# An opening with one array of scalars and single tiles, shifts on GpSimd, and the first w2 in quarters

## What is computed

```python
x = x + tanh(g_xattn[0]) * wkv(time_decay, time_first, k=layernorm(x), v=ctx_2048)
x = x + tanh(g_ffn[0])   * moe(layernorm(x), Wg, bg, W1, W2)

def wkv(...):                     # per batch and channel, over 256 positions
    aa, bb = decay * aa + exp(k) * v, decay * bb + exp(k)   # in a stable form
    y = (aa + exp(u + k) * v) / (bb + exp(u + k))           # with the sums before this position

def moe(x, Wg, bg, W1, W2):       # 2048 tokens, 4 experts, H = 2048
    logits = x @ Wg + bg          # the best two experts of each token, softmax over them
    for i in range(4):            # each expert takes the 512 tokens with the highest probability
        out[sel] += (gelu(x[sel] @ W1[i]) @ W2[i]) * p[sel]
```

## Time and profile before

| | us |
|---|---|
| median of 3 runs | 503.39 (503.37 to 503.77) |
| the profiled execution | 503.8 |
| its span, first to last instruction | 501.9 |
| TensorE busy | 419.5 |
| VectorE busy | 318.8 |
| ScalarE busy | 251.1 |
| GpSimd busy | 110.5 |

### The profile page before, as it was taken

The page is one execution under the profiler, slowest core; times in us unless marked ns, Lnnn a source line. Parts: engine busy times, 40 slices in busy tenths (PEclk is TensorE's granted clock), DMA queues, the critical chain, the costliest instruction groups (busy, mean ns, idle before and its releaser), DMA issues.

```text
span 501.9 us, 7234 instructions
## 1 busy us (share of the span) xinstructions
PE 419.5 (84%) x2012; PEld 200.3 (40%) x2012; DVE 318.8 (64%) x611; ACT 251.1 (50%) x374; POOL 110.5 (22%) x118
## 2 busy tenths in 40 slices
PE   0667877731168999999999999999999999999992
PEld 0433343310034444444444445444444444444440
DVE  4999999978747996173678419268833827771000
ACT  3736588970744445790444677154477615540000
POOL 1756636661030001311100221110031210001111
PEclk9997889985559999999999999999999999999998
DMA  7974012088530802918300471910075120000221
GB/s 225 347 308 179 17 42 86 31 304 292 210 85 0 335 0 82 359 9 288 100 0 1 164 275 21 355 21 0 1 255 184 21 27 16 0 0 1 35 29 21
DMA packets 24690, 59.30 MB, mean 118 GB/s; under 512 B 3040, under 2 KB 3040, under 8 KB 22624
## 3 DMA queue, kind: packets, MB, share of 16 engines
q1 hardware_dynamic: 19072, 50.68, 27.0%
q0 software_dynamic: 3584, 8.39, 8.4%
q10 hardware_dynamic: 2016, 0.02, 0.2%
HBM read 46.50 MB, written 12.58 MB: 118 GB/s over the span
## 4 chain that ended last, share of the span: by engine, by line
PE 70%; DVE 15%; ACT 6%; issue 3%; POOL 1%; DVEq 0%; ACTq 0%; POOLq 0%
PE ps L616 33%; PE ps L631 33%; DVE arena L990 5%; DVE arena L1009 2%; ACT arena L776 2%; PE ps L585 1%; DVE arena L1020 1%; DVE arena L1206 1%; ACT early L758 1%; PE ps L579 1%; DVE bn L967 1%; ACT rows L691 1%; ACT early L683 1%; DVE arena L1005 1%; ACT arena L707 1%
## 5 line engine op out<-in xcount | busy, mean ns | idle before, releaser
L616 PE MATMUL ps<-arena,early 128*128 128x512 f16 x768 | 166.4, 379 | 1.3 <-ACT arena L782 1.3
L631 PE MATMUL ps<-arena 128*128 128x512 f16 x768 | 167.4, 379 | 0.0
L616 PEld LDWEIGHTS ps<-arena,early 128*128 x768 | 75.0, 98 | 92.0 <-issue 2.1
L631 PEld LDWEIGHTS ps<-arena 128*128 128x128 f16 x768 | 74.9, 98 | 88.6
L797 ACT ACTIVATE arena<-ps,up 128x512 f32<-128x512 f32 x64 | 44.0, 687 | 84.0 <-PE ps L616 81.3
L1332 DVE TENSOR_SCALAR arena<-ps,yscale 128x512 f32<-128x512 f32 x16 | 12.0, 749 | 82.7 <-PE ps L631 61.3
L927 POOL DMA_INDIRECT result<-arena,idx x16 | 26.0, 1624 | 160.1 <-DVE arena L1332 158.5
L792 ACT ACTIVATE arena<-rows,down x64 | 45.6, 712 | 30.1 <-PE ps L631 30.1
L1317 DVE SCALAR_TENSOR_TENSOR arena<-arena,h_down 128x512 f32 x64 | 48.1, 751 | 9.7 <-DVE arena L1315 0.8
L1292 DVE SCALAR_TENSOR_TENSOR early<-w_raw,down,early 128x2048 f16<-128x2048 f32 x16 | 36.9, 2345 | 23.9 <-ACT early L758 22.3
L918 POOL DMA_INDIRECT arena<-xn_table,idx x16 | 17.1, 1069 | 158.5 <-DVE plist L1275 154.9
(11 more groups left out here) (160 smaller groups left out, 368.7 us busy)
## 6 DMA issues: line engine op xcount, KB each, us to landing
w_raw<-in_L_ffn_W SPq DMA_DIRECT2D x4, 4096.0 KB, 13.8
rows<-in_L_ffn_W SPq DMA_DIRECT2D x4, 4096.0 KB, 16.4
rows<-in_x SPq DMA_DIRECT2D x3, 1024.0 KB, 10.0
result<-rows SPq DMA_DIRECT2D x3, 1024.0 KB, 6.1
early<-in_ctx SPq DMA_DIRECT2D x4, 512.0 KB, 6.8
early<-in_ctx SPq DMA_DIRECT2D x2, 1024.0 KB, 6.6
xn_table<-arena SPq DMA_DIRECT2D x4, 512.0 KB, 3.5
xn_table<-arena SPq DMA_DIRECT2D x2, 1024.0 KB, 4.3
```

The lines of the kernel that those rows point to most:

```text
L616: last = nc.tensor.matmul(ps[:, PH[q], :], w[:, k, at], t[:, k, :], start=n == 0, stop=n == 3 * CT - 1)
L631: last = nc.tensor.matmul(ps[:, PY[s % 2], :], h[:, t, s * P:(s + 1) * P], w[:, t, :], start=t == 0 and n == 0, stop=t == HT - 1 and n == 2)
```

## The change

- **Opening.** All small inputs come in one array of 30 columns, laid out on the host, in one transfer on ScalarE's queue; context tiles 0 and 1 follow there one by one. SyncE loads the identity alone first, and the other constants later; x tiles 2 to 5 come in pairs, and SyncE waits for x tile 1 alone. Tiles 0 and 1 go singly: ScalarE makes their r as exp(-0.5 ln(var + eps)) (`first_scale`), VectorE their shift in one instruction (`first_shift`) and their product with the context (`first_m_rows`), between clearing the rows of `decay`. The table of Tanh is loaded by an instruction of its own. The increments of `start` move on ScalarE and VectorE from the beginning to just before the units.
- **decay in halves.** `set_decay` fills the first half of each row in the opening; the second halves follow in units 2 and 3, and unit 4's scan waits for them.
- **Statistics.** Those of tiles 2 to 5 move from the opening into units 0 and 1, others come earlier. `SHIFTS1` is gone: GpSimd makes the shifts itself, in `scales1`, with two more instructions for each of five groups of tiles.
- **w1's top first.** In `between` the four steps for w1's scale and the copy to `up` and `down` take rounds 0 to 4, the three steps on values rounds 5 to 7.
- **w2 in quarters.** Each quarter is loaded as soon as the rows in its place are stored; ScalarE sums quarters 0 and 1 before `w1_high` and 2 and 3 behind it.
- **Filler.** Two filler matmuls instead of three between the token tiles.

```diff
-STATS = {1: (6, 7), 2: (8, 9), 3: (10,), 4: (11, 12), 5: (13,), 8: (14,), 9: (15,)}
-SCALES1 = {2: 2, 5: 3, 9: 4}
-SHIFTS1 = {0: 1, 3: 2, 6: 3, 10: 4}
+STATS = {0: (2, 3), 1: (4, 5), 2: (6, 7), 3: (8, 9), 4: (10, 11), 5: (12, 13), 8: (14,), 9: (15,)}
+EDGE1 = (0, 2, 4, 6, 10, 14, 16)
+SCALES1 = {0: 1, 1: 2, 3: 3, 5: 4, 9: 5}
...
-            for g in range(NG):
-                sp.wait_ge(s_x1st[g], 16)
-            sp.dma_start(w2_raw[:, :, :], w2_v[:, 0]).then_inc(s_w2, 16)
+            for g in range(NG - 2):
+                store_x1(g)
+                store_xn2(g)
+            first_w2(0, (0, 1))
+            store_x1(NG - 2)
+            store_x1(NG - 1)
+            first_w2(1, (2,))
+            store_xn2(NG - 2)
+            store_xn2(NG - 1)
+            first_w2(2, (3,))
+            first_w2(3, (4,))
...
-                if r == 3:
+                if r == 0:
                     top_everywhere(1, 0, PW)
...
-                        keep_warm(3)
+                        keep_warm(2)
...
+            def first_scale(t):
+
+                act.wait_ge(s_mv1, t + 1)
+                nc.scalar.activation(var1[:, t:t + 1], mv1[:, t, 1:2], ACT.Ln, bias=eps[:, :]).then_inc(s_lnv, 1)
+                act.wait_ge(s_lnv, t + 1)
+                nc.scalar.activation(r1[:, t:t + 1], var1[:, t:t + 1], ACT.Exp, scale=-0.5).then_inc(s_r0, 1)
...
             for u in range(UNITS):
                 one_over_den(u)
+                if u in (2, 3):
+                    set_decay(2 * u - CT, 1)
+                    set_decay(2 * u - CT + 1, 1)
                 for t in ROWS_IN.get(u, ()):
                     exp_rows(t)
...
+            w2_magnitudes(0, (0, 1))
             w1_high(0)
-            w2_magnitudes(0)
+            w2_magnitudes(0, (2, 3))
...
+                nc.gpsimd.tensor_tensor(nb1[:, some], mv1[:, some, 0], r1[:, some], ALU.mult).then_inc(s_nb, 1)
+                pool.wait_ge(s_nb, 2 * g - 1)
+                nc.gpsimd.tensor_scalar(nb1[:, some], nb1[:, some], -1.0, -SHIFT, ALU.mult, ALU.add).then_inc(s_nb, 1)
...
-                if u < CT:
-                    dve.wait_ge(s_decay, u + 1)
+                if u < CT or u == CT:
+                    dve.wait_ge(s_decay, u + 1 if u < CT else 2 * CT)
```

More of the change, by code:

```diff
@@ L282, in program @@
         s_w2 = sem("w2_landed")
+        s_w2q = [sem(f"first_w2_quarter_{k}") for k in range(CT)]
         setup_d = sem("setup_dve")
@@ L382, in pair, with piece_of @@
             return both[:, first:last]
+        def piece_of(t):
+            return t if t < SPT else t // 2 + 1 if t < FIRST[2] else FIRST[2] // 2 + group_of(t) - 1
         def length(u):
@@ L666, in _ @@
-            nc.scalar.activation(chan[:, 1, :], chan[:, 0, :], ACT.Exp, scale=-1.0).then_inc(setup_a, 1)
-            act.wait_ge(setup_d, 4)
-            nc.scalar.activation(chan[:, 3, :], chan[:, 2, :], ACT.Exp, scale=-1.0).then_inc(setup_a, 1)
-            nc.scalar.activation(chan[:, 5, :], chan[:, 4, :], ACT.Exp).then_inc(setup_a, 1)
-            act.wait_ge(setup_a, 5)
-            def set_decay(k):
+            act.dma_start(small[:, :], scalars).then_inc(s_small, 16)
+            for t in range(SPT):
+                act.dma_start(c_sb[:, t:t + 1, :], c_v[:, t:t + 1, :]).then_inc(s_c0[t], 16)
@@ L674, in set_decay @@
+            def set_decay(k, part):
                 act.wait_ge(s_zero, k + 1)
-                v = decay[:, k, :].rearrange("p (b s) -> p b s", s=SEQ)[:, :, 1:SEQ]
+                v = decay[:, k, part * UN:(part + 1) * UN].rearrange("p (b s) -> p b s", s=SEQ)[:, :, 1:SEQ]
                 nc.scalar.activation(v, v, ACT.Identity, bias=chan[:, 1, k:k + 1]).then_inc(s_decay, 1)
             def exp_rows(t):
-                act.wait_ge(s_nb, 2 * (group_of(t) + 1))
+                if t < SPT:
+                    act.wait_ge(s_nb0, t + 1)
+                    act.wait_ge(s_r0, t + 1)
+                else:
+                    act.wait_ge(s_nb, 2 * max(g for g in range(len(EDGE1)) if EDGE1[g] <= t))
@@ L684, in exp_rows @@
                                      bias=nb1[:, t:t + 1], scale=r1[:, t:t + 1]).then_inc(s_ek, 1)
+            act.wait_ge(s_eps, 1)
+            first_scale(0)
+            nc.scalar.activation(chan[:, 0, :], td[:, 0, :], ACT.Exp).then_inc(setup_a, 1)
+            exp_rows(0)
+            act.wait_ge(setup_a, 2)
+            nc.scalar.activation(chan[:, 1, :], chan[:, 0, :], ACT.Exp, scale=-1.0).then_inc(setup_a, 1)
+            first_scale(1)
+            act.wait_ge(setup_d, 4)
+            nc.scalar.activation(chan[:, 3, :], chan[:, 2, :], ACT.Exp, scale=-1.0).then_inc(setup_a, 1)
+            nc.scalar.activation(chan[:, 5, :], chan[:, 4, :], ACT.Exp).then_inc(setup_a, 1)
+            exp_rows(1)
+            act.wait_ge(setup_a, 5)
+            for k in range(CT):
+                set_decay(k, 0)
+            start(act, c_tokhi, c_w1hi, c_w2hi, c_gelu, c_w2sum, c_w1sum)
             def take_rows(t):
@@ L767, in w1_magnitudes, with w2_magnitudes @@
                                          accum_out=wmax[:, 0, k:k + 1]).then_inc(c_w1sum, 1)
-            def w2_magnitudes(e):
-                act.wait_ge(s_w2, START + (e + 1) * 16)
+            def w2_magnitudes(e, parts=range(CT)):
                 act.wait_ge(c_hlo, START + e * HT)
-                for k in range(CT):
+                if not isinstance(e, int) or e > 0:
+                    act.wait_ge(s_w2, START + e * 16)
+                for k in parts:
+                    if isinstance(e, int) and e == 0:
+                        act.wait_ge(s_w2q[k], 16)
                     some = w2_raw[:, k * HT // CT:(k + 1) * HT // CT, :].rearrange("p a b -> p (a b)")
```

174 lines of the change are left out of this document (94 added, 80 removed).

## The result

The changed kernel took 496.28 us (median; 496.2 to 496.58), the kernel before beside it 503.38 us (503.33 to 503.77). The ratio is 0.986 with a 95% interval of 0.984 to 0.988: 7.1 us faster, where 6.7 were forecast. The profiled execution took 496.21 us with a span of 494.4.

The account below looks back on a forecast made before the run. The prediction took work ahead of TensorE's products as the only place to save: -4.7 + 0.5 + 1.6 - 1.6 - 2.6 = -6.8 us, giving 497.0 profiled and 496.7 median, range 494.6 to 499.0.

Parts of the forecast that it names:

- What bounds the kernel: Whole kernel: from 154 us only TensorE's products, untouched by the change, so any saving must come from the work ahead.
- Opening: Start to first scan: a shorter chain starts the scan at 11.9 instead of 16.52, minus 4.7 us (3.3 to 5.5).
- Units 0 to 3: First scan to unit 4's: each unit now has two statistics, plus 0.5 us, with GpSimd keeping pace.
- the wait: Unit 4's scan waits for ScalarE's two half rows of decay, plus 1.6 us (1.4 to 1.8).
- rival 1: Opening gives less: array late, increments not hidden, or GpSimd behind; 498.7 us, chance 0.22 together with rival 2.
- Units 4 to 10: Stage A: unit 5 gains a statistic, units 6 and 10 lose VectorE's stalled shifts, minus 1.6 us.
- rival 2: The stall of VectorE's shifts passes on and unit 6 stays long: 498.2 us, chance 0.22 together with rival 1.
- rival 3: Unit 4 has no decay wait, scan 4 held otherwise or ScalarE quicker: 495.1 us, chance 0.10.
- The end of stage A: Last units of stage A, bound by ScalarE, keep their work and shift whole: 0 us.
- Into stage C: Way to the last token tile: the list is late next, then the gather's landing decides, minus 2.6 us.
- Rival 4: Only the opening counts: TensorE starts the products at its lower clock, costing 2.5 us; 499.2 us, chance 0.05.
- Rival 5: Slower than before: quarter 1 of w2 lands late, delaying w1's high half; 507.2 us if at 138, chance 0.03.

Follow-up runs that it names:

- array_only: The kernel before with its six small loads replaced by the one array and nothing else moved: 503.46 us, ratio 1.000.
- scalars_apart: The changed kernel with its 30 columns of scalars loaded as six small transfers instead of one: 498.66 us, ratio 0.990.
- increments_first: The changed kernel with VectorE's 13 increments back at its beginning: 496.94 us, ratio 0.987.
- decay_early: The changed kernel with the second halves of decay filled in units 1 and 2 instead of 2 and 3: 494.88 us, ratio 0.983.
- shifts_only: The kernel before with GpSimd making the shifts of groups 1 to 4 itself, all else as before: 500.36 us, ratio 0.994.
- filler_3: The changed kernel with three filler matmuls instead of two between the last token tiles: 496.33 us, ratio 0.986.
- clears_by_gpsimd: decay_early with two of VectorE's four clearings of decay rows given to GpSimd at the start: 493.94 us, ratio 0.9815.
- w1_late: The changed kernel with w1's scale back in rounds 3 to 7, w2 still in quarters: 496.57 us, ratio 0.986.
- both_undone: The changed kernel with w1's scale late again and w2 loaded whole behind all stores, its sums behind w1's high half: 497.44 us, ratio 0.988.
- after_again: The changed kernel itself, unaltered, measured once more on the same chip: 496.49 us, ratio 0.986.

## Why the prediction was right, step by step

**What bounds the kernel** held: all of the gain lies ahead of the products, and those took 41.60 us for the first 192 and as long as before for the others.

**Opening, -4.7 predicted, -5.8 measured**, beyond the bounds of 3.3 to 5.5. This is the term that was mis-sized. The chain was the one predicted, in order and in its last part, but its first link was too long. I let the array land at 4.2 and put Tanh and the second table load behind it, 5.7. The array had landed by 3.43, 2.7 us behind its issue where I took 3.5, and Tanh started there, right behind the first table load, a link that I had left out; the second load ended at 4.93, 0.8 earlier than my 5.7. In `array_only`, where ScalarE waits for the same transfer, it landed 2.6 us behind its issue (1.17 to 3.76), so in after the table load was last by some 0.1 us only, and the 0.8 is the landing's size. From there to tile 1's shift the chain took 2.56 instead of 2.3, which gave 0.3 back, and VectorE's row 3.3 instead of 3.4. The last step gave 0.5: the small product took 0.10 where 0.45 was taken, and the scan's row begins 0.07 before the last clearing's ends, since the increments cost nothing. `scalars_apart` and `increments_first` confirm the two mechanisms by their size: 2.4 us for five more issues ahead of the table load, 0.95 for increments that stand in the open.

The Trainium skill ("ScalarE: Activation LUTs", What ACT_TABLE_LOAD costs) gives a table load as about 1283 ns and a drain of some 1380 ns beside it, 2.66 us for each switch to another set. The trace has the first figure, 1.28 us twice, but not the second: the Ln at 4.95 stands 0.02 behind the load's end, Tanh 0.01 behind its own, and the second load 0.02 behind Tanh. With both drains in the chain, scan 0 would stand an estimated 2.8 us later than it does; the measurement decides.

**Units 0 to 3, +0.5, and the wait, +1.6**: both held, with +0.6 and +1.5. Scan 0 to scan 4 is 16.20 (16.2 by the sum), the two half rows took 1.32 (1.34 taken), and `decay_early` took the wait out and got all of it back. GpSimd kept pace, as the slack of 2 us said. None of rival 1's three parts came: the array was early, the increments were hidden, and GpSimd wasn't behind.

**Units 4 to 10, -1.6**: +0.59 in unit 5, -1.59 in unit 6, -0.61 in unit 10, as taken. `shifts_only` excludes rival 2, and `decay_early` rival 3. Not every instruction of VectorE stalls beside GpSimd: statistics of 512 columns, which read one input, took 0.63 to 0.68 beside GpSimd's product.

**The end of stage A, 0 predicted, +0.3 measured.** I let these units, bound by ScalarE, shift whole, and had named it as a sign of being wrong if they didn't. They fell 0.3 us short of it: TensorE was at its lower clock there. The windows of after, and of before five us later, over the same work:

```profile
83.00:89.00 6.00, 5.88 (x22) 2.72 (x22) 5.86 (x12) 5.77 (x15) 3.51 (x4) 0.72 0.00 0
```

```profile
88.00:94.00 6.00, 5.48 (x26) 2.48 (x26) 5.86 (x11) 5.81 (x15) 3.25 (x4) 1.00 0.00 0
```

The granted clock is 0.72 against 1.00, and in after's chain TensorE's matmuls of L508, L531 and L519 stand with 3.6 us from 83.78 to 87.40, where before's chain, five us later, shows ScalarE. From the last scan to the first statistics behind it it is 5.92 in after and 6.03 in `decay_early`, 5.63 in before, 5.67 in `filler_3` and in `clears_by_gpsimd`. In `w1_late` it is 5.63, before's own, and there the granted clock is 1.00 from 83 to 89. All but before have the same code there. So the loss comes and goes with the clock from execution to execution; what makes TensorE fall in one and not in another wasn't tried.

**Into stage C, -2.6**: the size and its reason held, the last tile waits for its gather. But the parts were worth less than the sum lets think. `both_undone` shows 0.85 for the new order of w1 and w2 when the filler runs fast (1.2 by the medians), `w1_late` nothing for w1's scale alone, `filler_3` nothing for the shorter filler. They cover for each other, and the landing of the last gather is the floor under them all; the quarters alone weren't undone. "The first filler takes as long as before" was wrong for after's execution (3.98 against 5.33) and right for the one of `filler_3`, and it cost nothing for that same reason.

**Rival 4** didn't happen in after, but it is real one edit away: without the filler the clock fell in five of nine executions, for 1.7 us in the one that was profiled; I had said 2.5. **Rival 5** didn't happen either, but its cover was smaller than I wrote. I worked out 127.5, 134.3 and 119 from the list's end and the stores of before, though my own sum moved both 4.2 us earlier in the changed kernel; on one time axis they are 123.3, 130.1 and some 115, and the 507.2 would be some 511. Quarter 1 was awaited until 116.06, a little later than that 115, the last sum ended at 129.3, and the list's last instruction stood at 135.80: the cover was 6.5 us, of which `w1_late` used 5.0.

**The sum**: for the profiled execution I had 497.0, and it took 496.21; -1.1 of that is the opening, +0.3 the clock. For the median I took off 0.4 more, since before's profiled execution lay that much above its median; after's lies at its own, so 496.28 is only 0.4 below 496.7. That the median came so near is in part luck: the opening was off by more than its bounds allow, and the end of stage A and that 0.4 took part of it back.

## What to carry to other kernels

Write an opening down as one chain with every link in it, table loads and issue time included, since here the issuing of transfers and a table load, and not the landing, set when ScalarE could begin; and give each side job (a half row, a clearing) to the engine and place that has idle time, which was worth another 2.5 us here. Tiny instructions of VectorE that stand beside GpSimd's long products can last until the product ends (1.20 us instead of 0.17 here); look for them by their duration. Where several edits end under the same landing, undo them one at a time and together, and don't judge filler by one execution.

## What the runs showed of the hardware beyond that

- **GpSimd's first arithmetic** started at 8.79 (`scalars_apart`) to 11.18 us (`clears_by_gpsimd`) in all 14 traces, at 10.49 in before and 10.13 in after, behind 7.9 to 9.9 us of idle for which the trace names nothing, while its MEMSETs ran from 0.25 on, one of 1024 columns in 0.95. In `array_only` the first scan's chain waits for it, and in after it lies off the chain. Its cause is open.
- **Increments** run ahead of the engine: 13 of them in 1.1 us at 8.5 to 9.6 under two running instructions, and 0.95 to 1.2 us in the open at the start.
- **TensorE's clock** is not a property of a kernel alone: the same filler ran 3.98, 4.08 (`after_again`) and 5.33 us (`filler_3`), and one kernel without filler between the tiles gave two groups of times 1.8 us apart.
